# Scores turned by DMA transposes from SBUF to SBUF in place of TensorE transposes and ScalarE copies

## The chip, the cores and the metric

The kernel runs on one core of a Trainium2 chip. The metric is the device time of one execution in microseconds (us); lower is better. The profile shown below is of one execution of the kernel before the change.

## What is computed

Three parts follow one another on an input of 8 batches, 375 tokens and 64 channels: a token mixer, a retention layer, and a product-key attention. The change lies in the third part, which takes nearly all the time. Cut to what matters, for each head (8) and each batch (8), with n = 344 tokens:

```python
q = (x @ Wq_pk).reshape(b, n, 2, HEADS, 32)
sim = einsum(q, pk_keys)                  # two halves, 64 scores each per token and head
scores, idx = top_k(sim, 16)              # per half
score = scores[0][:, None] + scores[1][None, :]
final_scores, pk_idx = top_k(score, 16)   # of the 256 sums
kv_scores = softmax(final_scores)
k = einsum(kv_scores, keys_table[ind])    # weighted rows of a table of 4096 keys
v = einsum(kv_scores, values_table[ind])
out = causal_attention(q, k, v) @ Wo
```

The kernel does not gather table rows. It rebuilds the weight of each of the 4096 keys for each token (zero for those that are not chosen) and multiplies the whole table by these weights. For that it needs the two halves' scores with the keys on the partitions and the tokens along the free dimension, while the search for the largest ones has left them with the tokens on the partitions.

## The kernel before

The third part works through 64 items (8 heads by 8 batches; `i` is the item, `par` its parity, `slot` the parity of the head, `pair` the pair of batches). Every engine runs one loop over the items, written out by hand as 16 slots (`d` from 0 to 15, `NDC` = 16) per item; the order of an engine's work is the order of the code, and semaphores tie the engines together. An item's scores are prepared one or two items ahead.

In each slot TensorE issues the log weights of the slot that is `LEAD` = 5 ahead (L970: two matmuls, 128x344, f16, which select rows of the turned scores `X` and add them), and then the table sum of its own slot (L979, or L987 and L991 in every second slot). Between them ScalarE takes the exponential from PSUM to `W` (L1149), VectorE drops what lies under the threshold (L1436), and in every second slot ScalarE and GpSimd split `W` in a high and a low part (L1154, L1317). Because of the lead, the log weights that TensorE issues in slot 11 are the first ones of the next item; those of slot 15 are the fifth of the next item.

The scores of item i+1 come to the keys' side like this. In slot 6 of item i, ScalarE writes the high half of the centred scores to `spl` in f16 (`high_part`, L1140), and GpSimd the low half (`low_part`, L1311), which raises `low_step`. `spl` is 128 tokens by 3 token tiles (`TT`: 128, 128 and 88 tokens) by 5 blocks by 2 by 32. TensorE then turns them (`turn_scores`, L963) in two rounds of six transposes of at most 128x128 against an f16 identity `eye16`, into the PSUM bank `MID0`: the first round after slot 7, the second after slot 13. ScalarE copies each round from PSUM to `X` (`copy_turned`, L1144), in slots 8 and 14, and raises `x_ready`. TensorE waits for `x_ready` before the log weights that read a new half of `X`, before it overwrites the bank, and in `similarities`, which writes to the same bank.

`X` has two buffers (by parity) of four blocks of 344 columns. Block c // 8 serves chunk c of 32; a slot takes two chunks, so each block serves four slots of log weights.

SyncE issues the loads: at the start of a head the next head's table of 2 MB (L909) and two small query weights (L911), and in every second item a copy `xs` of the next pair's input from SBUF to SBUF (L932), after `sim_mm`.

Before the loop, item 0 goes through the same steps once (`turn_scores(0, 0)`, `turn_scores(0, 1)`, `copy_turned` twice), and TensorE issues five slots of log weights.

Of the kernel before, what the change touches and what calls it, by code (L numbers as in the profile page):

```python
# [18 lines left out]
F16 = mybir.dt.float16  # L19
# [10 lines left out]
H = 8  # L30
# [725 lines left out]
def product_key_attention(nc, ps, hT, x2T, const, pkw, wq, wo, tables, out):  # L756
# [14 lines left out]
    with ExitStack() as ctx:  # L771
        def sb(name, shape, dt=F32):
            return ctx.enter_context(nc.sbuf_tensor("k_" + name, shape, dt))

        def sem(name):
# [23 lines left out]
        eye16 = sb("eye16", [128, 128], F16)  # L799
# [20 lines left out]
        X = sb("X", [128, 2, 4, LOUT], F16)  # L820
# [21 lines left out]
        a_ready, clamped, low_step, high_ready, x_mm, x_ready = (  # L842
            sem("a_ready"), sem("clamped"), sem("low_step"), sem("high_ready"), sem("x_mm"), sem("x_ready"))
# [55 lines left out]
        with nc.Block() as block:  # L899

            @block.sync
            def _(sync):
# [17 lines left out]

                class Body:
# [6 lines left out]
                    @staticmethod  # L928
                    def item(i, slot, par, g, pair):
                        if par == 1:  # L930
                            wait_alone(sync, sim_mm, i + 3)
                            sync.dma_start(xs[:, :], x2T[:, bass.ds((pair + 2) % NPAIR, 1), :].rearrange("p a s -> p (a s)")).then_inc(xs_ready, 16)  # L932

                rounds(sync, Body)
                sync.wait_ge(xs_ready, 16 * (H * NPAIR + 1))

            @block.tensor
            def _(pe):
# [4 lines left out]
                def similarities(n, par, head, g=None):  # L943
                    if g is not None:
                        pe.wait_ge(x_ready, n * 2 - 2)
                        wait_alone(pe, xs_ready, g * 16 + 16)
                    for t, (t0, m) in enumerate(TT):
                        rhs = wf[:, par, head, :, :] if isinstance(head, int) else \
                            wf[:, par, bass.ds(head, 1), :, :].rearrange("p a b k -> p (a b) k")
                        mm = mm_(ps[0:m, MID0, 128 * t:128 * t + 128], (x2T[:, 0, :] if g is None else xs)[:, t0:t0 + m], rhs, start=True, stop=True)  # L950
                    mm.then_inc(sim_mm, 1)

                def turn_scores(n, r):

                    if r == 0:
                        pe.wait_ge(low_step, n + 1)
                        pe.wait_ge(sim_ready, n + 2)
                    else:
                        pe.wait_ge(x_ready, 2 * n + 1)
                    bank = ps[:, MID0, :].bitcast(F16)  # L960
                    for k in range(2):
                        for t, (t0, m) in enumerate(TT):
                            mm = tr_(bank[:, LOUT * k + t0:LOUT * k + t0 + m],  # L963
                                     spl[0:m, t, 2 * r + k:2 * r + k + 2, :, :].rearrange("p b x j -> p b (x j)"), eye16[0:m, 0:m])
                    mm.then_inc(x_mm, 1)

                def log_weights(i, par, d):
                    for k in range(2):
                        c = 2 * d + k
                        mm = mm_(ps[:, 2 * (d % 2) + k, 0:LOUT], sel[:, (c // 8) % 2, c % 8, :], X[:, par, c // 8, :], start=True, stop=True)  # L970
                    mm.then_inc(log_mm, 1)
# [90 lines left out]
                pe.wait_ge(cast_done, 4)  # L1062
# [4 lines left out]
                turn_scores(0, 0)  # L1067
                turn_scores(0, 1)
                pe.wait_ge(x_ready, 2)
# [6 lines left out]
                class Body:  # L1076
# [6 lines left out]
                    def item(i, slot, par, g, pair):  # L1083
                        nj = 1 - par
                        for d in range(NDC):
                            pe.wait_ge(w_done, i * NDC + (d + LEAD - 1))
                            if d + LEAD < NDC:
                                if d + LEAD == NDC // 2:
                                    pe.wait_ge(x_ready, i * 2 + 2)
                                log_weights(i, par, d + LEAD)  # L1090
                            else:
                                if d + LEAD == NDC:
                                    pe.wait_ge(x_ready, i * 2 + 3)
                                log_weights(i + 1, nj, d + LEAD - NDC)
# [10 lines left out]
                            if d == 7:  # L1105
                                turn_scores(i + 1, 0)
                            if d == 11:
                                turn_probabilities(i, nj)
                            if d == 13:
                                attention_output(i)  # L1110
                                turn_scores(i + 1, 1)
# [10 lines left out]
            def _(act):  # L1122
# [15 lines left out]
                def high_part(n):  # L1138
                    act.wait_ge(clamped, n * 2 + 2)
                    A(spl[:, :, :, 0, :], aS[:, :, :, :], ACT.Copy).then_inc(high_ready, 1)  # L1140

                def copy_turned(n, par, r):
                    act.wait_ge(x_mm, n * 2 + (r + 1))
                    A(X[:, par, 2 * r:2 * r + 2, :], ps[:, MID0, :].bitcast(F16)[:, 0:2 * LOUT], ACT.Copy).then_inc(x_ready, 1)  # L1144

# [59 lines left out]
                copy_turned(0, 0, 0)  # L1205
                copy_turned(0, 0, 1)
# [6 lines left out]
                class Body:  # L1213
# [5 lines left out]
                    def item(i, slot, par, g, pair):  # L1219
                        nj = 1 - par  # L1220
                        for d in range(NDC):
# [19 lines left out]
                            if d == 8:  # L1241
                                copy_turned(i + 1, nj, 0)
# [7 lines left out]
                            if d == 14:  # L1250
                                copy_turned(i + 1, nj, 1)
# [121 lines left out]
            def _(dve):  # L1373
# [111 lines left out]
                cast(eye16[:, :], "eye")  # L1485
# [194 lines left out]
```

## Time and profile before

| what | value |
|---|---|
| median of 3 runs | 2131.14 us (2130.26 to 2131.54) |
| the profiled execution's own time | 2144.47 us |
| its span, first to last instruction | 2142.4 us |
| TensorE (matmul) busy | 2034.5 us, 95% |
| VectorE busy | 1679.6 us, 78% |
| ScalarE busy | 1570.5 us, 73% |
| GpSimd busy | 1264.3 us, 59% |
| mean granted TensorE clock | 0.970 of full speed |

All durations of single instructions come from the profiled execution. In the rows, PE is TensorE's matmul side and PEld its weight load, DVE is VectorE, ACT ScalarE, POOL GpSimd, SPq the queue of SyncE. Matmuls overlap, so the chain of work, which counts each stretch of time once, tells what one of them costs on TensorE better than its own duration.

### The profile page before, as it was taken

The page shows a single profiled execution, that of the slowest core. Times are in us where ns is not written, and L with a number is a line of the kernel's source. Part 1 is how long each engine was busy: PE and PEld are TensorE (multiplying, and loading weights), DVE is VectorE, ACT ScalarE, POOL GpSimd, SP SyncE. Part 2 cuts the span into 40 slices and gives each one's busy share as a digit, 9 for nine tenths or more (in the row PEclk, how much of TensorE's full clock was granted, in tenths as well). Part 3 has the DMA queues.
Part 4 walks back from the last instruction along what each step waited for, and adds up shares of the span by engine and source line. Part 5 has one row for each costly group of instructions (what it writes and reads, how often), then busy time and mean ns, then how long its engine had stood idle before and what let it go on. Part 6 is the DMA issues. An engine that isn't in the chain of part 4 may idle for free.

```text
span 2142.4 us, 44765 instructions
## 1 busy us (share of the span) xinstructions
PE 2034.5 (95%) x12240; PEld 1555.0 (73%) x12240; DVE 1679.6 (78%) x5132; ACT 1570.5 (73%) x3253; POOL 1264.3 (59%) x1300
## 2 busy tenths in 40 slices
PE   5995859999999999999999999999999999999997
PEld 4892537777777777777777777777777777777776
DVE  4553458888888888888888888888888888888886
ACT  3563247778787878777878777787778777878776
POOL 2440106666666666666666666666666666666664
PEclk9997659999999999999999999999999999999999
DMA  3000020000100010001000100001000100010000
GB/s 93 1 0 0 1 91 5 3 3 0 44 4 3 3 44 3 3 3 43 4 3 3 40 7 3 3 3 44 3 3 0 44 3 3 3 43 4 3 3 17
DMA packets 11514, 31.68 MB, mean 15 GB/s; under 512 B 5184, under 2 KB 9408, under 8 KB 10173
## 3 DMA queue, kind: packets, MB, share of 16 engines
q1 hardware_dynamic: 8658, 30.36, 4.0%
q10 hardware_dynamic: 2795, 0.70, 0.1%
q14 instruction: 47, 0.39, 0.1%
q8 instruction: 14, 0.23, 0.0%
HBM read 24.55 MB, written 0.70 MB: 12 GB/s over the span
## 4 chain that ended last, share of the span: by engine, by line
PE 83%; DVE 1%; issue 1%; ACT 1%; DMA 0%; DVEq 0%; POOL 0%; SPq 0%; ACTq 0%; POOLq 0%
PE ps L979 27%; PE ps L970 15%; PE ps L987 15%; PE ps L991 7%; PE ps L1024 4%; PE ps L1042 3%; PE ps L950 2%; PE ps L963 2%; PE ps L1007 2%; PE ps L1034 2%; PE ps L1014 2%; PE ps L1001 1%; PE ps L1025 0%; DVE k_W L1436 0%; ACT k_W L1149 0%
## 5 line engine op out<-in xcount | busy, mean ns | idle before, releaser
L1317 POOL TENSOR_TENSOR k_W_low<-k_W,k_W_high 128x688 fp32r<-128x688 f32 x513 | 851.2, 1659 | 434.7 <-ACT k_W_high L1154 434.7
L1436 DVE SCALAR_TENSOR_TENSOR k_W<-ps,k_W 128x688 f32<-128x688 f32 x1028 | 887.7, 864 | 279.7 <-ACT k_W L1149 269.4
L1149 ACT ACTIVATE k_W<-ps 128x688 f32<-128x688 f32 x1029 | 766.7, 745 | 375.0 <-PE ps L970 358.7
L979 PE MATMUL ps<-k_W,k_tab 128*128 128x344 f32 x2048 | 676.8, 453 | 0.0
L970 PE MATMUL ps<-k_X,k_sel 128*128 128x344 f16 x2058 | 474.7, 312 | 16.0 <-DVE k_W L1436 8.9
L979 PEld LDWEIGHTS ps<-k_W,k_tab 128*128 128x128 f32 x2048 | 366.7, 190 | 127.1 <-issue 0.5
L1154 ACT ACTIVATE k_W_high<-k_W 128x688 fp32r<-128x688 f32 x513 | 396.0, 772 | 0.0
L987 PE MATMUL ps<-k_W_high,k_tab_high 128*128 128x344 f32 x1024 | 385.2, 379 | 0.0
L987 PE MATMUL ps<-k_W_high,k_tab_low 128*128 128x344 f32 x1024 | 324.1, 319 | 0.0
L970 PEld LDWEIGHTS ps<-k_X,k_sel 128*128 128x128 f16 x2058 | 151.7, 98 | 222.6 <-issue 99.5
L991 PE MATMUL ps<-k_W_low,k_tab_high 128*128 128x344 f32 x1024 | 244.4, 320 | 0.0
L987 PEld LDWEIGHTS ps<-k_W_high,k_tab_high 128*128 128x128 f32 x1024 | 193.6, 189 | 24.7
L987 PEld LDWEIGHTS ps<-k_W_high,k_tab_low 128*128 128x128 f32 x1024 | 193.7, 189 | 0.0
L991 PEld LDWEIGHTS ps<-k_W_low,k_tab_high 128*128 128x128 f32 x1024 | 177.2, 188 | 0.0
L1311 POOL TENSOR_TENSOR k_spl<-k_aS,k_spl 128x480 f16<-128x480 f32 x65 | 72.0, 1107 | 171.4 <-ACT k_spl L1140 171.4
L1024 PE MATMUL ps<-k_kv,k_qT 128*128 128x128 f32 (+2 forms) x390 | 107.8, 394 | 0.6 <-ACT k_vw L1169 0.6
L1278 POOL TENSOR_TENSOR k_cand<-k_top 128x192 f32<-128x192 f32 (+1 forms) x132 | 55.6, 446 | 75.0 <-DVE k_top L1383 75.0
L1144 ACT ACTIVATE k_X<-ps 128x688 f16<-128x688 f16 x130 | 95.5, 735 | 1.8 <-PE ps L963 1.8
L1423 DVE TENSOR_SCALAR k_aS<-k_aS 128x96 f32<-128x96 f32 x65 | 92.4, 1421 | 0.0
L1178 ACT ACTIVATE k_P<-ps,k_nmax 128x128 f32<-128x128 f32 (+2 forms) x195 | 87.2, 474 | 3.0 <-DVE k_nmax L1449 3.0
L214 POOL TENSOR_TENSOR P<-P,rz 95x756 f32<-95x756 f32 (+1 forms) x32 | 46.2, 1442 | 66.0 <-DVE rz L511 66.0
L1042 PEld LDWEIGHTS ps<-k_vw,k_PT 128*128 128x128 f32 (+2 forms) x780 | 83.0, 176 | 0.9 <-ACT k_PT L1184 0.9
(231 smaller groups left out, 2792.8 us busy)
## 6 DMA issues: line engine op xcount, KB each, us to landing
k_tab<-in_tables SPq DMA_DIRECT2D x9, 2048.0 KB, 7.2
k_xs<-x2T SPq DMA_DIRECT2D x33, 172.0 KB, 2.1
cst<-in_consts SPq DMA_DIRECT2D x1, 1024.0 KB, 19.0
wts<-in_weights SPq DMA_DIRECT2D x1, 896.0 KB, 13.0
cst<-in_consts SPq DMA_DIRECT2D x1, 874.5 KB, 16.7
xr<-in_xrows SPq DMA_DIRECT2D x1, 750.0 KB
xT<-in_xcols SPq DMA_DIRECT2D x1, 750.0 KB, 15.0
cst<-in_consts SPq DMA_DIRECT2D x1, 564.0 KB, 13.6
```

Source lines behind the costliest of these rows:

```text
L970: mm = mm_(ps[:, 2 * (d % 2) + k, 0:LOUT], sel[:, (c // 8) % 2, c % 8, :], X[:, par, c // 8, :], start=True, stop=True)
L979: mm = mm_(sums, tab[:, slot, at + k, :], W[:, d % RING, k, :], start=(d == 0 and k == 0), stop=(d == NDC - 1 and k == 1))
L987: mm_(sums, t[:, slot, at + k, :], W_high[:, q % SPLIT_RING, k, :], start=(d == 0 and k == 0 and t is tab_high), stop=False)
L991: mm = mm_(sums, tab_high[:, slot, at + k, :], W_low[:, q % SPLIT_RING, k, :], start=False, stop=(d == NDC - 1 and k == 1))
L1024: mm_(ps[0:m, bank, c0:c0 + keys], qT[:, pj, t0:t0 + m], kv[:, 0:keys], start=True, stop=False)
L1042: mm = mm_(ps[0:m, MID1, 64 * t:64 * t + 64], PT[0:kn, kt, t0 - k0:t0 - k0 + m], vw[0:kn, kt, :], start=(kt == 0), stop=(kt == t))
L1144: A(X[:, par, 2 * r:2 * r + 2, :], ps[:, MID0, :].bitcast(F16)[:, 0:2 * LOUT], ACT.Copy).then_inc(x_ready, 1)
L1149: A(W[:, d % RING, :, :], ps[:, 2 * (d % 2):2 * (d % 2) + 2, 0:LOUT], ACT.Exp).then_inc(e_done, 1)
L1154: A(W_high[:, split_at(d) % SPLIT_RING, :, :], W[:, d % RING, :, :], ACT.Copy).then_inc(high_done, 1)
L1317: G.tensor_tensor(W_low[:, q % SPLIT_RING, :, :], W[:, d % RING, :, :], W_high[:, q % SPLIT_RING, :, :].bitcast(F32), ALU.subtract).then_i ...
L1423: V.tensor_scalar(aS[:, :, 4, :], aS[:, :, 0, :], -NEG, FAR, ALU.min, ALU.max).then_inc(clamped, 1)
L1436: V.scalar_tensor_tensor(W[:, d % RING, :, :], ps[:, 2 * (d % 2):2 * (d % 2) + 2, 0:LOUT], 0.0, W[:, d % RING, :, :], ALU.is_ge, ALU.mult) ...
```

## The change

The six TensorE transposes of a round and ScalarE's copy go; SyncE issues six DMA transposes per item instead, which read `spl` and write `X`. One of them takes a token tile of 128 rows (96 for the last tile, whose 88 tokens are rounded up to a multiple of 16) with 256 columns of 2 bytes, and writes two blocks of `X` for these tokens. The three for the blocks 0 and 2 go first and raise `x_even`, then three for the blocks 1 and 3, which raise `x_odd`. `X` gets 352 columns per block, so that the 96 rows fit. TensorE waits for `x_even` in slot 11 and for `x_odd` in slot 15; ScalarE waits for both of the item before, before it overwrites `spl`. The identity `eye16` and its cast go.

```diff
-        X = sb("X", [128, 2, 4, LOUT], F16)
+        XW = 352
+        X = sb("X", [128, 2, 4, XW], F16)
@@ sync
+                def turn_scores(n, par):
+                    wait_alone(sync, low_step, n + 1)
+                    for odd, done in ((0, x_even), (1, x_odd)):
+                        for t, (t0, m) in enumerate(TT):
+                            rows = -(-m // 16) * 16
+                            sync.dma_start_transpose(X[:, par, odd::2, t0:t0 + rows],
+                                                     spl[0:rows, t, odd:odd + 4, :, :].rearrange("p b x j -> p (b x j)")).then_inc(done, 16)
+                turn_scores(0, 0)
...
                         if par == 1:
                             wait_alone(sync, sim_mm, i + 3)
                             sync.dma_start(xs[:, :], ...).then_inc(xs_ready, 16)
+                        turn_scores(i + 1, 1 - par)
@@ tensor
                     if g is not None:
-                        pe.wait_ge(x_ready, n * 2 - 2)
+                        pe.wait_ge(sim_ready, n)
-                def turn_scores(n, r):
-                    if r == 0:
-                        pe.wait_ge(low_step, n + 1)
-                        pe.wait_ge(sim_ready, n + 2)
-                    else:
-                        pe.wait_ge(x_ready, 2 * n + 1)
-                    bank = ps[:, MID0, :].bitcast(F16)
-                    for k in range(2):
-                        for t, (t0, m) in enumerate(TT):
-                            mm = tr_(bank[:, LOUT * k + t0:LOUT * k + t0 + m],
-                                     spl[0:m, t, 2 * r + k:2 * r + k + 2, :, :].rearrange("p b x j -> p b (x j)"), eye16[0:m, 0:m])
-                    mm.then_inc(x_mm, 1)
@@ tensor, before the loop
-                turn_scores(0, 0)
-                turn_scores(0, 1)
-                pe.wait_ge(x_ready, 2)
+                pe.wait_ge(x_even, 48)
+                pe.wait_ge(x_odd, 48)
@@ tensor, slot d
                             if d + LEAD < NDC:
-                                if d + LEAD == NDC // 2:
-                                    pe.wait_ge(x_ready, i * 2 + 2)
                                 log_weights(i, par, d + LEAD)
                             else:
                                 if d + LEAD == NDC:
-                                    pe.wait_ge(x_ready, i * 2 + 3)
+                                    pe.wait_ge(x_even, i * 48 + 96)
+                                if d + LEAD - NDC == NDC // 4:
+                                    pe.wait_ge(x_odd, i * 48 + 96)
                                 log_weights(i + 1, nj, d + LEAD - NDC)
-                            if d == 7:
-                                turn_scores(i + 1, 0)
...
-                                turn_scores(i + 1, 1)
@@ scalar
                 def high_part(n):
                     act.wait_ge(clamped, n * 2 + 2)
+                    if not isinstance(n, int):
+                        act.wait_ge(x_even, n * 48)
+                        act.wait_ge(x_odd, n * 48)
                     A(spl[:, :, :, 0, :], aS[:, :, :, :], ACT.Copy).then_inc(high_ready, 1)
-                def copy_turned(n, par, r):
-                    act.wait_ge(x_mm, n * 2 + (r + 1))
-                    A(X[:, par, 2 * r:2 * r + 2, :], ps[:, MID0, :].bitcast(F16)[:, 0:2 * LOUT], ACT.Copy).then_inc(x_ready, 1)
...
-                            if d == 8:
-                                copy_turned(i + 1, nj, 0)
...
-                            if d == 14:
-                                copy_turned(i + 1, nj, 1)
```

## Rows read from the trace of the kernel before

**Rows 1.** The page's busy time of each engine, with its share of the span.

```profile
PE 2034.5 (95%) x12240; PEld 1555.0 (73%) x12240; DVE 1679.6 (78%) x5132; ACT 1570.5 (73%) x3253; POOL 1264.3 (59%) x1300
```

**Rows 2.** Busy time by stretch, the middle of the loop, with clock and DMA.

```profile
core 0: us, PE busy (x) PEld busy (x) DVE busy (x) ACT busy (x) POOL busy (x), PEclk, DMA share, GB/s
560.00:1980.00 1420.00, 1412.06 (x8486) 1077.26 (x8485) 1195.83 (x3738) 1128.12 (x2227) 940.04 (x957) 1.00 0.03 12
```

**Rows 3.** The page's chain that ended last, shares by engine and by line.

```profile
PE 83%; DVE 1%; issue 1%; ACT 1%; DMA 0%; DVEq 0%; POOL 0%; SPq 0%; ACTq 0%; POOLq 0%
PE ps L979 27%; PE ps L970 15%; PE ps L987 15%; PE ps L991 7%; PE ps L1024 4%; PE ps L1042 3%; PE ps L950 2%; PE ps L963 2%; PE ps L1007 2%; PE ps L1034 2%; PE ps L1014 2%; PE ps L1001 1%; PE ps L1025 0%; DVE k_W L1436 0%; ACT k_W L1149 0%
```

**Rows 4.** Waits of TensorE from 340 to 2110 us: total, times, longest.

```profile
PE ps L970 <- DVE k_W L1436: 5.5, 6, 1.5
```

**Rows 5.** Groups by line: busy us, mean ns, then idle before and its releaser.

```profile
L970 PE MATMUL ps<-k_X,k_sel 128*128 128x344 f16 x2058 | 474.7, 312 | 16.0 <-DVE k_W L1436 8.9 <-DVE k_tab_low L1516 3.1 <-ACT k_X L1144 0.8
...
L1144 ACT ACTIVATE k_X<-ps 128x688 f16<-128x688 f16 x130 | 95.5, 735 | 1.8 <-PE ps L963 1.8
...
L963 PE MATMUL ps<-k_eye,k_spl 128*128 128x128 f16 (+1 forms) x780 | 62.0, 215 | 6.6 <-ACT k_sS L1130 5.8 <-ACT k_X L1144 0.8
```

**Rows 6.** The chain in order of time, one item: start, us, what.

```profile
1016.05 0.31 PE ps L963 x6
...
1026.29 0.31 PE ps L963 x6
```

**Rows 7.** Timeline of TensorE, two items: start, us, line, what.

```profile
1015.88 0.47 PE L963 MATMUL ps<-k_eye,k_spl 128*128 128x128 f16 x6
...
1020.46 0.46 PE L970 MATMUL ps<-k_X,k_sel 128*128 128x344 f16 x2
...
1027.88 0.46 PE L970 MATMUL ps<-k_X,k_sel 128*128 128x344 f16 x2
...
1043.88 0.47 PE L963 MATMUL ps<-k_eye,k_spl 128*128 128x128 f16 x6
...
1048.46 0.46 PE L970 MATMUL ps<-k_X,k_sel 128*128 128x344 f16 x2
```

**Rows 8.** Timeline of GpSimd: the low part, in the same two items.

```profile
1013.44 1.11 POOL L1311 TENSOR_TENSOR k_spl<-k_aS,k_spl 128x480 f16<-128x480 f32 x1 [2.66 <-ACT k_spl L1140]
...
1041.43 1.11 POOL L1311 TENSOR_TENSOR k_spl<-k_aS,k_spl 128x480 f16<-128x480 f32 x1 [2.66 <-ACT k_spl L1140]
```

**Rows 9.** Timeline of SyncE's queue from 1000 to 1060 us.

```profile
1001.71 0.34 SPq L909 DMA_DIRECT2D k_tab<-in_tables  x1
1002.25 1.17 SPq L911 DMA_DIRECT2D k_wqh<-in_wq  x2
1041.42 0.52 SPq L932 DMA_DIRECT2D k_xs<-x2T  x1
```

**Rows 10.** DMA: one queue's packets, MB, share; issues with KB each, median us to landing.

```profile
q10 hardware_dynamic: 2795, 0.70, 0.1%
...
k_tab<-in_tables SPq DMA_DIRECT2D x9, 2048.0 KB, 7.2
k_xs<-x2T SPq DMA_DIRECT2D x33, 172.0 KB, 2.1
```

**Rows 11.** Timeline before the loop: item 0's low part.

```profile
307.69 1.10 POOL L1311 TENSOR_TENSOR k_spl<-k_aS,k_spl 128x480 f16<-128x480 f32 x1 [1.43 <-ACT k_spl L1140]
```

**Rows 12.** The chain in order of time, before the loop.

```profile
310.63 0.74 PE ps L963 x6
...
312.99 0.75 ACT k_X L1144
313.74 0.05 issue
313.79 0.77 PE ps L970 x2
```

**Rows 13.** The chain from 560 to 1980 us: one of its three longest pieces without work.

```profile
1224.07 2.79 issue
```

More of the change, by code:

```diff
@@ L798, in product_key_attention @@
         sel = sb("sel", [128, 2, 8, 128], F16)
-        eye16 = sb("eye16", [128, 128], F16)
         eyeb = sb("eyeb", [128, 128], BF16)
@@ L841, in product_key_attention @@
             sem("ecs_ready"), sem("z_step"), sem("z_done"), sem("rz_z"), sem("gain_ready"))
-        a_ready, clamped, low_step, high_ready, x_mm, x_ready = (
-            sem("a_ready"), sem("clamped"), sem("low_step"), sem("high_ready"), sem("x_mm"), sem("x_ready"))
+        a_ready, clamped, low_step, high_ready, x_even, x_odd = (
+            sem("a_ready"), sem("clamped"), sem("low_step"), sem("high_ready"), sem("x_even"), sem("x_odd"))
         log_mm, e_done, w_done, main_done = sem("log_mm"), sem("e_done"), sem("w_done"), sem("main_done")
@@ L932, in item @@
                             sync.dma_start(xs[:, :], x2T[:, bass.ds((pair + 2) % NPAIR, 1), :].rearrange("p a s -> p (a s)")).then_inc(xs_ready, 16)
+                        turn_scores(i + 1, 1 - par)
                 rounds(sync, Body)
                 sync.wait_ge(xs_ready, 16 * (H * NPAIR + 1))
+                sync.wait_ge(x_even, 48 * (H * B + 1))
+                sync.wait_ge(x_odd, 48 * (H * B + 1))
             @block.tensor
@@ L969, in log_weights @@
                         c = 2 * d + k
-                        mm = mm_(ps[:, 2 * (d % 2) + k, 0:LOUT], sel[:, (c // 8) % 2, c % 8, :], X[:, par, c // 8, :], start=True, stop=True)
+                        mm = mm_(ps[:, 2 * (d % 2) + k, 0:LOUT], sel[:, (c // 8) % 2, c % 8, :], X[:, par, c // 8, 0:LOUT], start=True, stop=True)
                     mm.then_inc(log_mm, 1)
@@ L1061, in _ @@
                     mm.then_inc(y_mm0, 1)
-                pe.wait_ge(cast_done, 4)
+                pe.wait_ge(cast_done, 3)
                 pe.wait_ge(zeroed, 10)
@@ L1204, in _ @@
                 copy_similarities(1)
-                copy_turned(0, 0, 0)
-                copy_turned(0, 0, 1)
                 for d in range(LEAD):
@@ L1484, in _ @@
                 cast(sel[:, :, :, :].rearrange("p w c m -> p (w c m)"), "sel")
-                cast(eye16[:, :], "eye")
                 cast(eyeb[:, :], "eye")
```

## The prediction

> **What bounds the kernel now.** I read the page's busy times first, then the windows, the chain, the waits, and last the timelines of one item. The busy times put TensorE far ahead of the others [rows 1]. In the middle of the loop it leaves almost nothing free: 1412.06 of 1420 us, at the full clock, while VectorE has 1195.83, 84% [rows 2]. The chain agrees: 83% of the span is TensorE's, and the transposes of this change (L963) are 2% of it, ScalarE's copy is not named [rows 3]. In 1770 us TensorE waits for other engines 5.5 us in all [rows 4]. So in the loop TensorE's own work is the time: what is taken from its queue shortens the item, and what is put into its queue as a wait lengthens it.
>
> **What goes.** Per item TensorE issues two rounds of six transposes; the groups show them 780 times, that is 65 items (item 0 ahead of the loop, 64 in it) by 12, at 215 ns each [rows 5]. They overlap, so their price is read from the chain: 0.31 us for each round [rows 6]. 2 x 0.31 = 0.62 us per item, 64 x 0.62 = 39.7 us. An item is 1043.88 - 1015.88 = 28.00 us long [rows 7] and would be 27.38.
> ScalarE's copy goes as well, 130 of 735 ns, 95.5 us busy [rows 5]. In the loop I count it at nothing, because what hides it is TensorE: nobody's chain has it there [rows 3]. The cast of the identity is one small instruction ahead of the loop beside the other casts; the two new waits of ScalarE before the high part are for transposes of an item earlier, landed some 18 us before. Both at nothing.
> Could VectorE eat the gain? Its work is 0.84 x 28.00 = 23.6 us per item, against 27.38: no.
>
> **What comes in, and its deadlines.** GpSimd's low part ends at 1013.44 + 1.11 = 1014.55 [rows 8]; only then may SyncE issue. The first log weights that read the new blocks start in slot 11, at 1020.46 [rows 7], which the removed round brings forward by 0.31: the even three transposes have 1020.46 - 0.31 - 1014.55 = 5.60 us. The next item gives the same: 1048.46 - 0.31 - 1042.54 = 5.61 [rows 7, 8]. The odd three are wanted in slot 15, 1027.88 - 0.62 - 1014.55 = 12.71 us after the low part. The low part itself follows slot 6 of TensorE, so this room does not grow when TensorE is held up. A wait in slot 11 stops everything queued behind it: these log weights, the table sums behind them, and with them, slots later, ScalarE's exponentials and VectorE's thresholds. Hence the whole sum for the loop: with T the time from the low part to the landing of the even three, the item changes by max(0, T - 5.60) - 0.62, and 64 times that is the loop. The sign turns at T = 6.22.
>
> **The size of T.** No DMA transpose is in this trace. Bounds from the nearest rows:
> Below: the even three carry (128 + 128 + 96) x 512 bytes = 176 KB, as much as one `xs` copy from SBUF to SBUF, 172 KB, which lands 2.1 us after its issue [rows 10]. T can't be less.
> With three issues one after another: a plain issue holds SyncE for 0.34, 0.52 or 1.17 / 2 = 0.585 us [rows 9]. Two issues of 0.6 and then the landing of the third: 1.2 + 2.1 = 3.3 us.
> Above, no overlap at all: 3 x 2.1 = 6.3 us, or with 0.6 of issue before each landing 3 x 2.7 = 8.1 us.
> Above, by pieces: the code rounds rows to 16, so a piece written to one partition is probably 16 values, 32 bytes; 128 partitions x 22 groups of 16 tokens x 2 blocks = 5632 pieces. The queue of small packets (0.70 MB / 2795 = 250 bytes) used 0.1% of 16 engines' span: 0.001 x 16 x 2142.4 / 2795 = 12 ns each, 6 to 18 within the rounding [rows 10]. 5632 / 16 x 12 ns = 4.2 us, and with the landing 6.3 us (4.2 to 8.4).
> Above, by single values: 90,112 / 16 x 12 ns = 68 us for half an item.
> I take the middle between the overlapped 3.3 and the edge of 5.60, T = 4.5, which is 1.2 us per transpose and 2.1 for the last: the operation most like it is the `xs` copy, same memory on both sides, same bytes, same queue. In the loop, T is then covered by the four slots of TensorE work between. The odd three land at 5 x 1.2 + 2.1 = 8.1 us, inside 12.71.
>
> The Trainium skill speaks against it. First the rows: plain issues take 0.34 to 0.585 us [rows 9], and a TensorE transpose 0.05 us on the chain, 0.31 / 6 [rows 6]. The skill ("VectorE: DVE Perf Modes", The three transpose paths) gives 1309 ns for a crossbar transpose of 128x128 in bf16 and, in its rules, TensorE wherever PSUM will do as target. If blocks went one behind the other at that figure, the even half, 704 / 128 = 5.5 blocks, would be an estimated 7.2 us, and the loop 64 x (1.6 - 0.62) = 63 us longer instead of 39.7 shorter. No row here shows it. "DMA: Bandwidth & Descriptors" (Latency and other measured facts) has 261 GB/s for DMA transposes, by which 176 KB would be an estimated 0.7 us; the two pull apart.
>
> **Other parts.** SyncE's queue: the 2 MB table is issued at 1001.71 and lands 7.2 us later, 5.6 us before the low part ends [rows 8 to 10]. The `xs` copy is issued at 1041.42 and has left SyncE at 1041.94, 0.6 us before the low part's end at 1042.54; its tail of 1 us may share the engines. Both at nothing; if the cover goes, one `xs` per two items delays T by at most 2.1 us.
> Ahead of the loop there is no cover. Item 0's low part ends at 308.79 [rows 11]; TensorE's first log weights start at 313.79, after two rounds and two copies [rows 12]. Now all six must have landed: 308.79 + 8.1 = 316.9, so +3.1 us (3.3 to 5.60 for T gives 5.1 to 10.9 for six, +0.1 to +5.9).
> The clock: pauses of 2.79 us in the chain left it at 1.00 [rows 2, 13], so short waits in slot 11 would not lower it.
>
> **Sum.** -39.7 + 3.1 = -36.6 us. The profiled execution took 2144.47 us itself and would take 2107.9; the median of the runs shown is 13.3 us under it, so I forecast 2131.14 - 36.6 = 2094.5 us.
>
> **The rivals.**
> A. *Hidden*, as above: 2094.5, with 2088 to 2097 as its own range (T from 2.1 to 5.60). Chance 0.44. For it: 5.6 and 12.7 us of room against 2.1 for a copy of the same size. Against it: six issues, not one.
> B. *Late by less than the gain*: T between 5.60 and 6.1, for instance 5.85: 64 x (0.25 - 0.62) = -24, +6 ahead of the loop: 2113. Chance 0.10.
> C. *Slower: the transposes are not overlapped.* Place: TensorE's wait in slot 11. Price: each transpose delays the next by x, T = 3x; it decides from x = 2.07 us on. With x = 2.4 (between 2.1 and 2.7): T = 7.2, 64 x (1.6 - 0.62) = +63, and ahead of the loop 6 x 2.4 = 14.4, +9: 2203. With 2.1 it is 2144. With 2.7 the odd half ends it, 16.2 against 12.71: 64 x (3.5 - 0.62) = +184 and +11: 2326. Chance 0.30. The skill's 1309 ns, above, would come out at the same 7.2 us. Against it: no plain issue here is over 0.6 us.
> D. *Slow by small pieces*: T = 6.3, 64 x (0.7 - 0.62) = +5, and ahead of the loop twice 4.2 and 2.1, 10.5 us, +5.5: 2142. The packet price is known to a factor, so 0.07 slower, 0.03 within the band.
> E. *The change does not do what it says*: the transposes are done value by value. Six would take some 135 us per item, 64 x 107 = 6800 us more. Chance 0.03. The skill ("VectorE: DVE Perf Modes", same section) has strided transposes 19 times slower than those of the crossbar; no row shows either.
> F. *The freed time is taken by another engine*, VectorE at 84% first: no change, 2131. Chance 0.03.
>
> **The numbers.** What a measurement of this kernel can tell from no change is about 0.2%, 4 us. Faster: A and B, 0.54. The same: F and a part of D, 0.06. Slower: C, the rest of D, and E, 0.40. The forecast is A's 2094.5. The range for 8 in 10 starts at A's floor less 2 us, 2086, and must take in most of C and D: up to 2260, which leaves out the upper quarter of C and E, about 0.11.
>
> **What would show it.** Right: TensorE's busy share in the middle stays at 99%, no wait of L970 on a DMA, items 27.4 us apart, issues of transposes on SyncE's queue under 1.75 us each, (5.60 - 2.1) / 2. Wrong: a row of waits of TensorE for `X` by a DMA, 64 times, in slot 11, and items longer than 28.0 us; then T is over 6.22, and the length of one issue on SyncE's queue against its landing tells C from D. A wait in slot 15 would mean six transposes over 12.7 us. If instead VectorE appears as releaser of L970 in every item, it is F.

## The result, and the profile after

| | median us | lowest to highest | ratio to before, 95% interval |
|---|---|---|---|
| before (4 runs) | 2131.22 | 2130.26 to 2131.54 | |
| after (4 runs) | 2079.81 | 2078.45 to 2082.11 | 0.9751, 0.973 to 0.9773 |

The change makes the kernel 51.4 us faster; the forecast was 36.6 us faster, 2094.5, and the range began at 2086. The sign and the likeliest case (A, *Hidden*) came true, the size did not: 14.8 us of the gain were not in the sum.

Two of the executions timed for the experiments below lie far outside all others, one of copy8_back (4073.3 us) and one of before (6759.2 us); the medians hardly move by them and the ratios leave them out.

The profiled execution of after took 2082.11 us itself, with a span of 2080.3. That is 62.1 us less span than before's, but 8.8 us of it lie ahead of item 0's low part, where the two kernels do the same work but for one cast (the low part starts at 298.89 us, before at 307.69 [rows 11]). Spans are therefore not compared below; items are.

First the page of after, its busy times [rows 1] and the chain's shares [rows 3]:

```profile
PE 1967.2 (95%) x11460; PEld 1520.1 (73%) x11460; DVE 1707.0 (82%) x5131; ACT 1503.6 (72%) x3123; POOL 1264.5 (61%) x1300
...
PE 81%; issue 2%; DVE 1%; DMA 0%; POOL 0%; ACT 0%; SPq 0%; DVEq 0%; POOLq 0%; ACTq 0%
```

Then the windows over the same stretch as [rows 2], and the waits of TensorE in the loop, from 320 to 2050 us [rows 4]:

```profile
core 0: us, PE busy (x) PEld busy (x) DVE busy (x) ACT busy (x) POOL busy (x), PEclk, DMA share, GB/s
560.00:1980.00 1420.00, 1413.79 (x8144) 1091.43 (x8143) 1259.01 (x3864) 1111.08 (x2192) 973.35 (x993) 1.00 0.10 26
```

```profile
PE ps L970 <- DVE k_W L1425: 6.5, 7, 1.5
PE ps L970 <- DMA k_X<-k_spl: 1.4, 2, 1.2
```

TensorE is as full as before, 1413.79 of 1420 us, so the gain in the loop comes out of what these rows count as TensorE's work; a part of it will prove to have been short waits. Its matmuls are shown waiting for the new transposes twice in 64 items. VectorE has gone from 84% to 89%, and only a part of this is that the items are shorter. Over the whole execution it is busy 27.4 us longer for as many instructions (1707.0 against 1679.6), and one small one makes this up. Before:

```profile
L1410 DVE TENSOR_SCALAR k_small<-k_small 128x3 f32<-128x3 f32 x65 | 27.3, 420 | 0.0
```

The same instruction is L1399 after, with 859 ns in place of 420 (its row stands further below); 65 x 0.44 is 28.5 us.

How much an item gained is read from GpSimd's timeline, low part to low part [rows 8]:

```profile
1341.72 1.11 POOL L1300 TENSOR_TENSOR k_spl<-k_aS,k_spl 128x480 f16<-128x480 f32 x1 [2.65 <-ACT k_spl L1139]
1368.81 1.11 POOL L1300 TENSOR_TENSOR k_spl<-k_aS,k_spl 128x480 f16<-128x480 f32 x1 [2.65 <-ACT k_spl L1139]
```

1368.81 - 1341.72 = 27.09 us. The median over all items is 27.09, where before has 28.01: 0.92 us less per item, and the removed rounds are only 0.62 of it. From the first low part to the last, before takes 1801.64 us and after 1749.57, 52.07 less.

**The deadlines.** SyncE's timeline after the low part at 1368.81, the new tile's view (issues: shortest, median, longest ns; then issue to landing in us), and TensorE's log weights in slots 11 and 15 [rows 7]:

```profile
1370.02 7.60 SPq L927 DMA_TRANSPOSE k_X<-k_spl  x6
```

```profile
L927 SPq DMA_TRANSPOSE k_X<-k_spl x390: 1167/1242/2449, 300.1 to 2056.0; - x195
...
DMA to landing us min/median/max: 2.3/2.4/4.2
```

```profile
1375.40 0.46 PE L970 MATMUL ps<-k_X,k_sel 128*128 128x344 f16 x2
...
1382.41 0.46 PE L970 MATMUL ps<-k_X,k_sel 128*128 128x344 f16 x2
```

The low part ends at 1368.81 + 1.11 = 1369.92. Six issues take 7.60 us, 1.27 from one to the next. The third begins at 1370.02 + 2 x 1.27 = 1372.56 and lands 2.4 later, at 1374.96: T = 5.0 us. Slot 11 comes at 1375.40, so the room is 5.48 us and half a microsecond of it is left. The odd three land at 1370.02 + 5 x 1.27 + 2.4 = 1378.8, 8.9 us after the low part; slot 15 comes 12.5 after it.

**Ahead of the loop** (timeline: item 0's low part, the six issues, TensorE's first log weights; [rows 11, 12]):

```profile
298.89 1.09 POOL L1300 TENSOR_TENSOR k_spl<-k_aS,k_spl 128x480 f16<-128x480 f32 x1 [1.43 <-ACT k_spl L1139]
300.08 7.70 SPq L927 DMA_TRANSPOSE k_X<-k_spl  x6
...
309.09 1.31 PE L970 MATMUL ps<-k_X,k_sel 128*128 128x344 f16 x4 [13.69 <-DMA k_X<-k_spl]
```

From the end of the low part, 299.98, to the first log weights it is 9.1 us, where before had 5.0: 4.1 later, forecast 3.1. This is where the transposes are in the open in every execution. Item 0 itself, low part to low part, is 34.54 us long against 31.59.

So T, the room and the price of a round came out near the forecast. What is left to explain is the rest of the 0.92 us.

### The profile page after: what moved, and what is told of

Its sections match the earlier page's. It is cut to its first block, busy times and chain, and to the rows that moved or that the text cites. A ratio compares the mean times of both kernels' runs of the same rounds, so it can differ in the third digit from the quotient of the medians.

```text
span 2080.3 us, 43530 instructions
## 1 busy us (share of the span) xinstructions
PE 1967.2 (95%) x11460; PEld 1520.1 (73%) x11460; DVE 1707.0 (82%) x5131; ACT 1503.6 (72%) x3123; POOL 1264.5 (61%) x1300
## 3 DMA queue, kind: packets, MB, share of 16 engines
q1 hardware_dynamic: 112658, 53.84, 9.5%
## 4 chain that ended last, share of the span: by engine, by line
PE 81%; issue 2%; DVE 1%; DMA 0%; POOL 0%; ACT 0%; SPq 0%; DVEq 0%; POOLq 0%; ACTq 0%
PE ps L979 27%; PE ps L987 15%; PE ps L970 15%; PE ps L991 8%; PE ps L1024 4%; PE ps L1042 3%; PE ps L964 2%; PE ps L1034 2%; PE ps L1007 2%; PE ps L1014 2%; PE ps L1001 1%; PE ps L1025 0%; DMA k_X<-k_spl 0%; SPq L927 0%; DVE k_W L1425 0%
## 5 line engine op out<-in xcount | busy, mean ns | idle before, releaser
L1144 ACT ACTIVATE k_W<-ps 128x688 f32<-128x688 f32 x1029 | 765.4, 744 | 390.2 <-PE ps L970 372.8
L970 PE MATMUL ps<-k_X,k_sel 128*128 128x344 f16 x2058 | 472.8, 311 | 27.9 <-DMA k_X<-k_spl 15.1
L1149 ACT ACTIVATE k_W_high<-k_W 128x688 fp32r<-128x688 f32 x513 | 395.4, 771 | 0.0
L970 PEld LDWEIGHTS ps<-k_X,k_sel 128*128 128x128 f16 x2058 | 170.8, 99 | 217.0 <-issue 77.1
L1042 PE MATMUL ps<-k_vw,k_PT 128*128 128x64 f32 (+2 forms) x780 | 81.8, 255 | 0.7 <-ACT k_PT L1179 0.7
## 6 DMA issues: line engine op xcount, KB each, us to landing
cst<-in_consts SPq DMA_DIRECT2D x1, 874.5 KB, 16.5
```

The lines of the kernel that those rows point to most:

```text
L1042: mm = mm_(ps[0:m, MID1, 64 * t:64 * t + 64], PT[0:kn, kt, t0 - k0:t0 - k0 + m], vw[0:kn, kt, :], start=(kt == 0), stop=(kt == t))
L1144: A(W[:, d % RING, :, :], ps[:, 2 * (d % 2):2 * (d % 2) + 2, 0:LOUT], ACT.Exp).then_inc(e_done, 1)
L1149: A(W_high[:, split_at(d) % SPLIT_RING, :, :], W[:, d % RING, :, :], ACT.Copy).then_inc(high_done, 1)
```

## The experiments

The measure in all of them is the item: the median distance of two low parts, which single executions can tell to a few hundredths of a microsecond. Before was timed on the same chip as each kernel; its medians were 2133.78, 2131.79 and 2129.94 us in the three groups of kernels.

| kernel | item us | item 0 us | median us | ratio to before, 95% interval |
|---|---|---|---|---|
| before | 28.01 | 31.59 | 2131.22 | |
| after | 27.09 | 34.54 | 2079.81 | 0.9751, 0.973 to 0.9773 |
| copies_back | 27.32 | 35.70 | 2092.05 | 0.9815, 0.9768 to 0.9862 |
| copy8_back | 27.33 | 35.82 | 2092.75 | 0.9795, 0.9749 to 0.9841 |
| rounds_back | 27.72 | 35.71 | 2121.57 | 0.9951, 0.9925 to 0.9977 |
| both_back | 27.92 | 35.60 | 2129.27 | 0.9973, 0.9945 to 1.0 |
| short_copy | 27.78 | 30.31 | 2116.81 | 0.9935, 0.992 to 0.9949 |
| one_extra | 28.06 | 35.84 | 2144.55 | 1.007, 1.0036 to 1.0104 |
| odd_at_11 | 30.63 | 34.54 | 2344.40 | 1.0978, 1.0938 to 1.1017 |
| split_cols | 31.8 | 42.9 | 2373.68 | 1.1139, 1.1095 to 1.1184 |
| no_fast_mode | 27.12 | 34.59 | 2080.40 | 0.9753, 0.9722 to 0.9784 |
| fused | 27.57 | 36.18 | 2106.04 | 0.9894, 0.9877 to 0.9911 |
| lead | 27.12 | 31.72 | 2074.34 | 0.9743, 0.9729 to 0.9758 |
| lead_fused | 27.55 | 32.17 | 2104.09 | 0.9883, 0.9866 to 0.99 |

### Which removed part gave what: four kernels

Each puts back a part of what was removed, beside the DMA transposes. The copies write to a scratch tile that nobody reads, at the places of the old ones and for as long (727 ns against 735), and TensorE waits for them in `similarities` only, not ahead of the log weights and the second round as before; the rounds write to the bank `MID0` and nobody reads them.

```diff
+                def copy_scratch():
+                    A(scr[0:88, :, :], ps[0:88, MID0, None, 0:LOUT].to_broadcast([88, 2, LOUT]), ACT.Copy).then_inc(scr_done, 1)
@@ scalar, slot 8, and in copies_back and both_back slot 14
+                                copy_scratch()
@@ tensor, rounds_back and both_back: after slots 7 and 13
+                                turn_rounds(i + 1, 0)
...
+                                turn_rounds(i + 1, 1)
```

`turn_rounds` is the old `turn_scores` with its 12 TensorE transposes, without the wait for the copy.

> Left out: nothing; added to the changed kernel are two ScalarE copies per item (688 elements, PSUM to a scratch tile that nobody reads), in slots 8 and 14, where the removed copies were. Theory 1 (the removed copies made VectorE's thresholds late, and TensorE waited for them in pieces of 0.1 us): the item grows from 27.09 to 27.37 us, the time from 2079.8 to about 2098. Rival 2 (ScalarE's copies cost nothing, and a round of transposes costs TensorE 0.45 us and not 0.31): item 27.09, time 2080, no change.

> The changed kernel with only the copy of slot 8 put back, into a scratch tile. Theory 1, from the chain's pieces before (L970 takes 0.42 and 0.38 us in slots 11 and 12, 0.29 after the change): the item grows by 0.22 us to 27.31, time about 2094; the copy in slot 14 is worth the other 0.06 to 0.10 us. Rival 2: no change, 2080.

> The changed kernel with the two rounds of six TensorE transposes per item put back after slots 7 and 13, into the PSUM bank that they had, without any copy out of it; the scores still come by DMA. Theory 1: the item grows by 2 x 0.31 = 0.62 us to 27.71, time 2079.8 + 39.7 = 2119.5. Rival 2: by 0.91 us to 28.00, time about 2138.

> The changed kernel with both put back, the TensorE rounds and the ScalarE copies (into a scratch tile), the DMA transposes kept beside them. If the two removals are all of the gain, the item is 28.0 us as before, and the time 2138 (2131 and the 4 us ahead of the loop). If the DMA transposes help or hurt by themselves (contention with other engines for the memory), it is apart from 28.0 by that much.

Measured: the rounds alone make the item 27.72 - 27.09 = 0.63 us longer, what [rows 6] said. The copies alone make it 27.32 - 27.09 = 0.23 us longer, and the copy of slot 8 alone the same 0.24; on top of it the copy of slot 14 costs nothing, where the expectation gave it 0.06 to 0.10. In the chain it does lengthen slot 1's log weights (0.34 us in copies_back, 0.29 after), but those of slot 3, which wait for VectorE in any case, shorten by as much. Both together give 27.92 of before's 28.01.

Where the copy's 0.23 us lie shows in TensorE's chain, in order of time. Before, slots 11 and 12:

```profile
1020.50 0.42 PE ps L970 x2
...
1022.44 0.38 PE ps L970 x2
```

After, the same slots:

```profile
1375.56 0.29 PE ps L970 x2
...
1377.36 0.29 PE ps L970 x2
```

copies_back (its log weights are at L972):

```profile
1019.77 0.41 PE ps L972 x2
...
1021.69 0.38 PE ps L972 x2
```

The same two matmuls take 0.42 and 0.38 us of the chain before, 0.29 and 0.29 after, and 0.41 and 0.38 as soon as the copy is back. With the rounds back and no copy, both are 0.29. The timeline of copies_back tells why:

```profile
1017.32 0.73 ACT L1144 ACTIVATE k_scr<-ps 88x688 f16<-88x688 f32 x1
1017.94 0.74 ACT L1149 ACTIVATE k_W<-ps 128x688 f32<-128x688 f32 x1
1018.71 0.87 DVE L1434 SCALAR_TENSOR_TENSOR k_W<-ps,k_W 128x688 f32<-128x688 f32 x1 [0.87 <-ACT k_W L1149]
1019.71 0.11 PEld L972 LDWEIGHTS ps<-k_X,k_sel 128*128 128x128 f16 x2 [0.49 <-issue]
1019.72 0.46 PE L972 MATMUL ps<-k_X,k_sel 128*128 128x344 f16 x2
```

The copy (L1144 here) stands in front of an exponential (L1149). VectorE has been idle for 0.87 us until that exponential ends at 1018.68, and its threshold ends at 1019.58. TensorE's log weights in slot 11 wait for `w_done` of just that threshold (`w_done` up to `d + LEAD - 1`, in slot 11 that of slot 14), and start at 1019.72. So TensorE, which is the bound, waited about a tenth of a microsecond in two slots of every item for a chain that began with ScalarE's copy. Its table sums of the slot before were still ending in the meantime, and so the chain and the waits of its matmuls book the time as matmul and not as idle. The rows of its weight loads (PEld) do show it. Slot 11 before and after, with the idle time ahead in brackets:

```profile
1020.46 0.11 PEld L970 LDWEIGHTS ps<-k_X,k_sel 128*128 128x128 f16 x2 [0.51 <-issue]
1375.40 0.10 PEld L970 LDWEIGHTS ps<-k_X,k_sel 128*128 128x128 f16 x1 [0.19 <-issue]
```

**The last 0.06 us.** Rounds and copies make 0.86 of the 0.92 us. The rest lies in slot 3, where before and short_copy (below) have a piece without work ahead of the log weights that the kernels without `x_ready` hardly have; first before, then after:

```profile
1033.78 0.05 issue
1033.83 0.46 PE ps L970 x2
1361.18 0.01 issue
1361.19 0.47 PE ps L970 x2
```

Short_copy has 0.11 us there and rounds_back 0.01, and their items, 27.78 and 27.72, differ by the same 0.06. In slot 3 before and short_copy also wait for `x_ready` (`d + LEAD == NDC // 2`), which the change moved to slot 15 as `x_odd`. That this wait is the cause fits, but no kernel took it out alone.

### The copy's price from the other side: short_copy

Before, with its two copies cut to 8 of 344 columns. TensorE's rounds and all waits stay; `X` is zero but for these columns, so the log weights are not the reference's.

```diff
-                    A(X[:, par, 2 * r:2 * r + 2, :], ps[:, MID0, :].bitcast(F16)[:, 0:2 * LOUT], ACT.Copy).then_inc(x_ready, 1)
+                    A(X[:, par, 2 * r:2 * r + 2, 0:8], ps[:, MID0, :].bitcast(F16)[:, 0:16], ACT.Copy).then_inc(x_ready, 1)
```

> The kernel before with ScalarE's two copies per item cut from 344 to 8 columns per block (the other columns of X stay zero, so the weights are not the reference's). Theory 1 (a copy on ScalarE cost TensorE 0.23 to 0.29 us per item through late thresholds): the item falls from 28.01 to about 27.75 us, time about 2114. Rival (their cost lay in something else of the change): item 28.01, time 2131.

Measured: 27.78, 0.23 us less than before, and the pieces of slots 11 and 12 in its chain are 0.29 and 0.29. The same figure from both kernels, by adding the copy to the one and by taking it from the other. 64 x 0.23 = 14.7 us, against 14.8 that were missing. That the two agree so closely is luck: further gains of 4.5 us and losses of about as much, listed further below, cancel.

### The edge of the room: one_extra

One more transpose of 128x256, to a tile that nobody reads, is issued ahead of the even three.

```diff
+                    for k in range(1):
+                        sync.dma_start_transpose(X_extra[:, :, :],
+                                                 spl[:, k, 0:4, :, :].rearrange("p b x j -> p (b x j)")).then_inc(x_extra, 16)
```

> The changed kernel with one more DMA transpose (128 rows by 256 columns, into a scratch tile that nobody reads) issued ahead of the even three of every item. After the change an issue takes 1.24 us, the even three land T = 5.0 us after the low part, and TensorE wants them 5.5 us after it. Theory (the wait in slot 11 is the deadline, and it has 0.5 us to spare): T = 6.25, the item grows by 0.75 to 0.8 us to 27.9, time about 2130. Rival (the DMA queue overlaps more than its issues show, or the room grows when TensorE is late): under 0.2 us per item, time under 2093.

The chain, from the end of the low part on (L928 is the extra one; the even three are L933, of which the chain names two issues and the landing of the last):

```profile
1119.70 1.17 SPq L928
...
1120.92 1.24 SPq L933
...
1122.21 1.24 SPq L933
...
1123.49 2.38 DMA k_X<-k_spl
```

and the waits of TensorE, 320 to 2100 us:

```profile
PE ps L977 <- DMA k_X<-k_spl: 52.8, 63, 2.1
```

T is 1119.45 to 1125.87, 6.42 us, where 6.25 was expected. Over the room of 5.48 that is 0.94, and the item grew by 28.06 - 27.09 = 0.97. So the rule of the forecast, that the item grows by max(0, T - room), holds to 0.03 us, and one issue more turns 51 us of gain into a loss of 0.7%: after stands 0.5 us from its edge and 1.4 us of T from no gain at all.

### The wait put too early: odd_at_11

TensorE waits for the odd three in slot 11 already, with the even three.

```diff
-                                if d + LEAD - NDC == NDC // 4:
                                     pe.wait_ge(x_odd, i * 48 + 96)
```

> The changed kernel with TensorE's wait for the odd three moved from slot 15 to slot 11, beside the wait for the even three. Theory: all six land 0.1 + 5 x 1.27 + 2.4 = 8.8 us after the low part, against 5.5 us of room: the item grows by 3.35 us to 30.4, time about 2294. Rival (the odd half is hidden anyway): no change, 2080.

Measured: 30.63 us per item and 2344 us, 50 us more than the estimate. The wait itself was right: six landings take 8.87 us (1119.61 to 1128.48), 3.4 over the room of 5.48, and the median item grew by 3.54, 0.2 more than the 3.35 expected, which is 12 of the 50 us. The rest is the clock, as the windows of one item show (the last three columns are the granted clock, the DMA share and GB/s):

```profile
492.00:494.00 2.00, 1.37 (x6) 0.62 (x4) 1.97 (x10) 2.00 (x8) 0.76 (x1) 1.00 0.15 33
494.00:496.00 2.00, 0.00 (x0) 0.00 (x0) 1.33 (x8) 0.41 (x1) 1.51 (x1) 0.85 0.26 57
496.00:498.00 2.00, 1.28 (x5) 1.18 (x6) 0.00 (x0) 0.45 (x1) 0.28 (x2) 0.50 0.01 0
498.00:500.00 2.00, 2.00 (x11) 1.94 (x10) 0.88 (x1) 0.60 (x2) 0.00 (x0) 0.50 0.00 0
500.00:502.00 2.00, 2.00 (x7) 1.38 (x6) 0.68 (x2) 1.08 (x2) 0.00 (x0) 0.50 0.00 0
502.00:504.00 2.00, 2.00 (x13) 1.58 (x12) 1.44 (x8) 1.55 (x4) 1.59 (x1) 0.95 0.00 0
```

TensorE stands still for over 3 us. Its granted clock falls to 0.50, 1.2 GHz, before it works again, and stays there for some 6 us, 5 of them behind the pause. This did not happen in every item. The median item, 30.63, has the wait alone at the full clock; 20 of the other 63, item 0 left out, have a lower mean clock (0.90 to 0.95) and took 31.99 to 33.95 us, and the 39 us that they took beyond the median are the missing time. Over the whole run the mean clock is 0.955, against 0.975 in after and 0.977 in one_extra, whose waits are 0.84 us long on average.

### Price per instruction or per byte: split_cols

Each transpose of 256 columns is cut into two of 128, twelve per item with the same bytes in all.

```diff
-                            sync.dma_start_transpose(X[:, par, odd::2, t0:t0 + rows],
-                                                     spl[0:rows, t, odd:odd + 4, :, :].rearrange("p b x j -> p (b x j)")).then_inc(done, 16)
+                            for c in (odd, odd + 2):
+                                sync.dma_start_transpose(X[:, par, c, t0:t0 + rows],
+                                                         spl[0:rows, t, c:c + 2, :, :].rearrange("p b x j -> p (b x j)")).then_inc(done, 16)
```

> The changed kernel with each DMA transpose of 256 columns cut in two of 128 columns, 12 per item instead of 6, the same bytes. If an issue costs 1.24 us whatever it moves, the even half needs 5 x 1.27 + 2.4 + 0.1 = 8.8 us, the item is 30.4 us and the time 2294. If an issue costs by what it moves (0.62 us each), T stays at 5.0 us or less and the time at 2080. Between them, with 0.8 us each: T = 6.5, item 28.1, time 2144.

The tile's view:

```profile
L928 SPq DMA_TRANSPOSE k_X<-k_spl x780: 1093/1232/2457, 293.0 to 2346.1; - x195
...
DMA to landing us min/median/max: 2.2/2.4/4.5
```

Half the columns, the same issue (1232 ns against 1242) and the same landing. So at these two widths T is 0.1, plus 1.27 for each instruction but the last, plus 2.4, whatever the bytes; with six in the even half it is 0.1 + 5 x 1.27 + 2.4 = 8.9 us. The wait of 8.9 - 5.5 = 3.4 us in slot 11 and the twelfth landing (0.1 + 11 x 1.27 + 2.4 = 16.5 us against 12.5 plus that wait, 0.6 late) give items of 27.09 + 3.4 + 0.6 = 31.1 us; the expected 30.4 had left the twelfth landing out. 31 of the 63 items behind item 0 kept the full clock, and their median is 31.15. The other 32 have a mean clock of 0.95 and a median of 31.99, so the clock pushes the median of all to 31.8. By this price fewer and wider transposes should help, which wasn't tried.

### Could VectorE give more: no_fast_mode, fused, lead_fused

With TensorE as the bound to a tenth of a microsecond, VectorE's small instructions at the end of a slot came into question. One of them lasts five times as long as its twin of the same shape (after, groups by line: busy us, mean ns):

```profile
L1399 DVE TENSOR_SCALAR k_small<-k_small 128x3 f32<-128x3 f32 x65 | 55.9, 859 | 0.0
...
L1400 DVE TENSOR_SCALAR k_small<-k_fin 128x3 f32<-128x3 f32 x65 | 10.1, 155 | 0.0
```

no_fast_mode writes it, its twin and the clamps as operations of another form with the same result; fused does the two and the three that follow (L1406) with two instructions in slot 3.

```diff
@@ no_fast_mode
-                    V.tensor_scalar(small[:, AM, :], small[:, AM, :], -DELTA, None, ALU.mult).then_inc(top_step, 1)
+                    V.scalar_tensor_tensor(small[:, AM, :], small[:, AM, :], -DELTA, small[:, AM, :], ALU.mult, ALU.min).then_inc(top_step, 1)
@@ fused
+                    V.scalar_tensor_tensor(small[:, FLOOR, :], small[:, AM, :], -DELTA, fin[:, :, 15], ALU.mult, ALU.add).then_inc(floor_step, 1)
+                    dve.wait_ge(floor_step, n + 1)
+                    V.scalar_tensor_tensor(small[:, MX, :], fin[:, :, 0], -80.0, small[:, FLOOR, :], ALU.add, ALU.max).then_inc(mx_ready, 1)
```

> A version that may beat both: the changed kernel with VectorE's four tensor_scalar instructions from SBUF to SBUF in floors and clamp_scores (0.88 and 1.40 us long where they run beside GpSimd's W_low, 0.16 and 0.23 us ahead of the loop) written as scalar_tensor_tensor with the same result. In the trace after, the one in floors ends when GpSimd's instruction ends, and the threshold behind it lets TensorE's slot 4 wait 0.17 us. Theory: they no longer wait for GpSimd, slot 4 takes 0.29 us, the item 26.9, the time 2079.8 - 64 x 0.2 = about 2067. Rival (the form of the instruction changes nothing): item 27.09, 2080.

> The changed kernel with floors folded into threshold: two scalar_tensor_tensor instructions of 128x3 in slot 3 in place of two in slot 1 and three in slot 3, same result. Theory: the one in slot 1 waits for GpSimd and lets TensorE's slot 4 wait; without it slot 4 takes 0.29 us and not 0.47, the item 26.9 us, time about 2067. Rival (the new one in slot 3 waits as long, beside the next W_low, or slot 4's wait has another cause): item 27.09, 2080.

> Both of the last two together, the version meant to beat both kernels. Theory: item 26.9 us and 4 us less ahead of the loop: about 2063. Rival: 2076 if the fold gives nothing.

The other form changed nothing: 860 ns, item 27.12. Fused was slower, 27.57, though it issues three instructions fewer. Its timeline:

```profile
1013.81 1.68 POOL L1306 TENSOR_TENSOR k_W_low<-k_W,k_W_high 128x688 fp32r<-128x688 f32 x1 [0.21 <-ACT k_W_high L1149]
...
1013.89 1.62 DVE L1401 SCALAR_TENSOR_TENSOR k_small<-k_small,k_fin 128x3 f32<-128x3 f32 x1
...
1015.54 0.16 DVE L1403 SCALAR_TENSOR_TENSOR k_small<-k_fin,k_small 128x3 f32<-128x3 f32 x1
```

Three elements per partition last 1.62 us and end within 0.02 us of GpSimd's split of 688 columns; the like of it a moment later takes 0.16. The instructions that fused removed (L1406, 128x1, 258 ns) did not do this in the same place. TensorE then waits 66 times for VectorE, 36.0 us. The theory that fewer instructions shorten this piece fell; what ties the small instruction to GpSimd's stays open. The expectations call the place slot 4; by the code's count it is slot 3. Lead_fused, which was to reach 2063 us, came to 27.55 us per item and 2104.09: it keeps the loss of fused.

### The exposed place: lead

Only item 0 is turned the old way, with TensorE's rounds and ScalarE's copies ahead of the loop; the DMA transposes start with item 1.

```diff
-                turn_scores(0, 0)
...
-                pe.wait_ge(x_even, 48)
-                pe.wait_ge(x_odd, 48)
+                bank = ps[:, MID0, :].bitcast(F16)
+                for r in range(2):
...
+                    mm.then_inc(x_mm, 1)
+                pe.wait_ge(x_ready, 2)
@@ scalar
+                for r in range(2):
+                    act.wait_ge(x_mm, r + 1)
+                    A(X[:, 0, 2 * r:2 * r + 2, 0:LOUT], ps[:, MID0, :].bitcast(F16)[:, 0:2 * LOUT], ACT.Copy).then_inc(x_ready, 1)
```

> The changed kernel, where only item 0's scores, ahead of the loop, are turned as before by TensorE and copied by ScalarE. Ahead of the loop nothing covers the six DMA transposes: low part to first log weights 9.1 us after, 5.0 before. Theory: 4 us less, 2076; items unchanged at 27.09. Rival (something else is as late there): 2080.

The chain ahead of the loop (round, copy, round, copy, first log weights at L969):

```profile
294.53 0.75 PE ps L1075 x6
...
296.89 0.75 ACT k_X L1212
...
297.69 0.77 PE ps L969 x2
```

Item 0's low part ends at 292.68, the log weights start 5.0 us later, as before, and item 0 is 31.72 us long instead of 34.54: 2.8 us back. The other items are 27.12 us against 27.09, so that from the first low part to the last it takes 1747.86 us, 1.7 less than after. At 2074.34 us (2073.35 to 2078.05) it has the lowest median measured, but of the 8.5 us between the two profiled spans 7.3 lie ahead of item 0's low part, where the changes do nothing. It was not timed side by side with after, and the intervals of the two ratios overlap. So that it beats before is shown; that it beats after rests on these 1.7 us of one execution each.

## Why the prediction was right in sign and too small

**The step that failed**, as it was put: ScalarE's copy, "In the loop I count it at nothing, because what hides it is TensorE: nobody's chain has it there [rows 3]". It costs 0.23 us per item, all of it by the copy in slot 8, shown from both sides (copy8_back and short_copy). The reading of the chain was at fault: here it went back through TensorE's own queue and named no releaser while matmuls overlapped, and waits of 0.13 and 0.09 us vanished in the ends of the matmuls before. The trace of before had the signs of it: the same pair of log weights at 0.29 us in most slots, at 0.42 and 0.38 in slots 11 and 12, three and four slots behind the copy, and 0.51 us of idle time ahead of slot 11's weight loads.

**The sum as it should have been**, per item:

| term | forecast | measured | from |
|---|---|---|---|
| the two rounds | -0.62 | -0.63 | rounds_back against after |
| ScalarE's copies | 0 | -0.23 | copies_back, copy8_back, short_copy |
| the wait in slot 11 | 0 | 0 in the median item | T 5.0, room 5.48 |
| slot 3, cause not shown | 0 | -0.06 | 0.92 in all; short_copy against rounds_back |
| loop, 64 items | -39.7 | -58.9, less the longer ones | low parts |
| ahead of the loop | +3.1 | +4.1 to the first log weights | after |

64 x 0.92 = 58.9 us, and first to last low part gives 52.07: item 0, which holds the late start, grew by 2.95 where the others shrank by 0.92, which is 3.9 of the difference, and five more items of after are longer than their like, one of them 28.50, four 27.28 to 27.45, 2.4 us in all. Each of these five has a landing of 3.0 to 4.2 us. What delays those landings wasn't tried. Against the forecast that makes 14.7 us more gain by the copies, 4.5 by the 0.01 and the 0.06, 0.8 less in item 0 and 2.4 less in the five items, 16.0 in all; 14.8 were measured, and 1.2 are left to rounding and to the differences between executions.

**What was removed from TensorE**: right to 0.01 us, by the chain's 0.31 per round and not by the transposes' own 215 ns [rows 5, 6].

**The room**: 5.60 forecast, 5.48 found. **T**: 4.5 forecast, 1.2 us from one transpose to the next and 2.1 for the landing; 5.0 found, 1.27 (of which 1.24 the issue) and 2.4. Nearer to the edge than thought, still inside. The Trainium skill ("VectorE: DVE Perf Modes", The three transpose paths) gives 1309 ns for a DMA transpose of 128x128 in bf16. The trace agrees within 6% if this is read as the price of one instruction on its queue (1232 ns for 128x128), and speaks against reading it as a price per block (1242 ns for 128x256). The same page of the Trainium skill (Rules for kernel authors) advises TensorE if PSUM will do as target. Here the scores had to end in SBUF, PSUM was a stop on the way, and the case does not speak against the advice; it shows what the way through TensorE and ScalarE cost, 0.63 and 0.23 us per item.

**The rivals.** C needed a pitch of 2.07 us; it was 1.27. Its mechanism is real: one_extra brought it about with one instruction more, and the item followed its arithmetic. B did not occur. D, small pieces, is false in its outcome: per item there are (112,658 - 8,658) / 65 = 1600 packets, 800 for a half, where D counted 5632 for a half (8,658 is the same queue before; after, packets, MB and share):

```profile
q1 hardware_dynamic: 112658, 53.84, 9.5%
```

E is false by the same count. F is false, since the item shrank by more than the freed 0.62 us. The sign that the prediction named for F, VectorE as releaser of L970 in every item, does not tell: among the matmuls VectorE is named seven times in 1730 us, but waits as short as those above stand in no such row.

**The clock**: "short waits in slot 11 would not lower it" held for the waits of 0.84 us in one_extra (0.977). Waits of 3.4 us did lower it, in 20 items of odd_at_11. The upper end of the range, 2260, means waits of an estimated 2.5 us per item ((2260 - 2131 - 9) / 64 + 0.62, with 9 us ahead of the loop as in C), less than the 2.79 of [rows 13] that left it at 1.00. Only C's time with x = 2.7, which has 3.5 us of waiting per item, may have been too low; no run has just these waits.

## What to carry to other kernels

When one engine is full, compare equal instructions of it slot by slot in the chain, and look at the idle time ahead of its weight loads: here two pairs that lasted a tenth of a microsecond longer than their like were waits, and what they waited for began on an engine at 73%. So an operation off the chain is not free until such pieces have been looked at. Price DMA transposes of such widths by their number and not by their bytes, and give each consumer its own semaphore and its own deadline: here three transposes, 5.0 us, fit in 5.48, a fourth did not, and waiting for all six at the first deadline made the kernel 10% slower than before. Where there is no cover (ahead of a loop), keep the path with the shorter latency.

## What the runs showed of the hardware

- A DMA transpose from SBUF to SBUF held SyncE's queue for 1.23 us with 128 columns and 1.24 us with 256, against 0.34 to 0.585 for plain issues [rows 9], and landed 2.4 us after its issue began.
- With pauses of TensorE of over 3 us the granted clock went to 0.50 in 20 of 63 items of odd_at_11 and in the item shown stayed there some 6 us; with pauses of 0.84 us on average in every item of one_extra it did not fall, nor with one of 2.79 us before [rows 13].
- A VectorE instruction of 128x3 lasted 0.155 to 0.16 us alone and, beside GpSimd's 128x688, 0.42 us before, 0.86 after and 1.62 in fused; in fused it ended within 0.02 us of GpSimd's.
- The transposes move 226 bytes per packet on average, (53.84 - 30.36) MB over 112,658 - 8,658 = 104,000 packets (the same queue before: 8,658 packets, 30.36 MB, 4.0%), and took an estimated 17 ns of one DMA engine each, (0.095 x 2080.3 - 0.040 x 2142.4) x 16 / 104,000 in us: a DMA share of 0.10 in the middle of the loop against 0.03 before.
